# Row constants, modulation weights and the first context's keys requested ahead of the step that uses them, in a four-layer transformer kernel

## What is computed

```python
# layer 0
m = silu(mod) @ w_ada + b_ada                        # nine vectors of 256: shift, scale, gate
x = x + (window_attn(ln(x) * (1 + sc) + sh) @ w_so + b_so) * g_msa
x = x + (topk_cross(ln(x) ..., ctx @ w_kv + b_kv) @ w_co + b_co) * g_mca     # 16 largest of 77 scores
x = x + (silu(h @ m1a) * (h @ m1b) @ w_m2 + b_m2) * g_mlp
# layer 1 (512 tokens at a time)
evidence = softmax(nx @ Wq @ (proto @ Wk).T / 16) @ (proto @ Wv)
combined = concat([nx, evidence, anchor])            # the anchor is the condition, the same for all tokens
x = x + sigmoid(gate(combined)) * (sum_e p_e * expert_e(combined) @ out_w + out_b)
# layer 2
mod = cond @ adaLN_W + adaLN_b
x = x + g_msa * (masked_attn(rope(q), rope(k), v) @ attn_out_W)
x = x + g_x * (cross(xc @ cq_W, ctx @ ck_W, ctx @ cv_W, mask) @ co_W)
x = x + g_mlp * (gelu(xm @ W1 + b1) @ W2 + b2)
# layer 3
c = silu(c) @ W_mod + b_mod
x = x + gate_a * (attn(qkv + b_qkv) @ W_proj + b_proj)
x = x + (cross(...) @ W_cproj + b_cproj)
x = x + gate_m * (gelu(h @ W_mlp1 + b_mlp1) @ W_mlp2 + b_mlp2)
```

## Time and profile before

| | us |
|---|---|
| median of three runs | 3021.17 (3016.11 to 3022.32) |
| the profiled execution | 3020.91 |
| its span in the trace | 3019.6 |
| TensorE busy | 2471.6 (82%) |
| VectorE busy | 1911.2 (63%) |
| ScalarE busy | 1209.9 (40%) |
| GpSimd busy | 258.0 (9%) |

### The profile page before, as it was taken

How to read it: one execution, slowest core, us unless ns; L and a number is a source line. 1 busy time by engine, 2 the same in 40 slices (tenths; PEclk the granted TensorE clock), 3 DMA queues, 4 the chain that set the end, 5 groups by cost and what they waited for, 6 DMA issues and landing times.

```text
span 3019.6 us, 37681 instructions
## 1 busy us (share of the span) xinstructions
PE 2471.6 (82%) x13127; PEld 1252.1 (41%) x13127; DVE 1911.2 (63%) x5983; ACT 1209.9 (40%) x2250; POOL 258.0 (9%) x252
## 2 busy tenths in 40 slices
PE   5787558787699778999788989987889978889677
PEld 2455324454355353444344445442234332234335
DVE  5655857587533466556767766647777668776445
ACT  2323313343222222444434545433546626556324
POOL 2011010001210010000020010010011010000101
PEclk9798679798899796999999999997989989999869
DMA  4545141000000030000232110042220032110120
GB/s 156 146 131 150 50 128 63 20 20 13 7 7 10 30 93 17 22 11 22 72 102 75 33 27 12 12 126 70 59 42 11 28 93 80 40 25 8 56 54 14
DMA packets 151650, 161.34 MB, mean 53 GB/s; under 512 B 33471, under 2 KB 120978, under 8 KB 151196
## 3 DMA queue, kind: packets, MB, share of 16 engines
q1 hardware_dynamic: 151460, 158.94, 18.3%
HBM read 98.04 MB, written 60.19 MB: 52 GB/s over the span
## 4 chain that ended last, share of the span: by engine, by line
PE 59%; DVE 25%; ACT 5%; DMA 4%; issue 3%; POOL 2%; SPq 2%; DVEq 0%; ACTq 0%; POOLq 0%
PE bank L1097 8%; PE bank L1562 7%; PE bank L1069 6%; PE bank L1044 6%; PE bank L1583 5%; DVE max L1170 3%; PE bank L2037 3%; PE bank L722 3%; PE bank L1073 3%; DVE bank L1167 2%; PE bank L2214 2%; DVE k_stack L1334 2%; PE bank L1482 2%; PE bank L2039 1%; PE bank L663 1%
## 5 line engine op out<-in xcount | busy, mean ns | idle before, releaser
L1111 ACT ACTIVATE work<-bank 128x512 f32<-128x512 f32 (+1 forms) x1216 | 702.6, 596 | 721.7 <-PE bank L1073 296.6
L1167 DVE CUSTOM_DVE_ANT_0 bank<-bank,weights 128x512 f32<-128x512 f32 x512 | 349.1, 703 | 196.1 <-PE bank L1044 194.8
L1044 PE MATMUL bank<-k_stack,q_stack 97*128 97x512 bf16 x896 | 368.4, 413 | 89.8 <-DVE max L1167 43.4
L1170 DVE TENSOR_REDUCE max<-bank 128x1 f32<-128x512 f32 x512 | 340.8, 685 | 127.0 <-PE bank L1044 125.5
L1069 PE MATMUL bank<-q_stack,k_stack 99*128 99x512 bf16 x896 | 349.3, 393 | 15.2 <-ACT work L1111 13.0
L1562 PE MATMUL bank<-hT,weights 128*128 128x512 f32 x512 | 267.6, 623 | 15.5 <-ACT work L1608 6.8
L1044 PEld LDWEIGHTS bank<-k_stack,q_stack 97*128 97x128 bf16 x896 | 90.4, 101 | 298.6 <-DVE max L1167 118.9
L1073 PEld LDWEIGHTS bank<-ident_b,weights 128*128 128x128 bf16 x2048 | 161.0, 99 | 122.6 <-issue 15.7
L1073 PE MATMUL bank<-ident_b,weights 128*128 128x128 bf16 x2048 | 202.0, 221 | 0.0
L1583 PE MATMUL bank<-weights,work 128*128 128x256 f32 x768 | 197.8, 386 | 0.0
L1413 POOL TENSOR_TENSOR x<-x,work 128x512 f32<-128x512 f32 x64 | 82.0, 1282 | 1108.1 <-DVE work L1401 1103.6
(11 more groups left out here) (239 smaller groups left out, 3696.0 us busy)
## 6 DMA issues: line engine op xcount, KB each, us to landing
q_stack<-parts_q SPq DMA_DIRECT2D x60, 384.0 KB, 3.9
...
```

Of the source, the lines that this page charges most:

```text
L1044: m = pe.e.matmul(bank.ap[:, :], self.q(g)[0:MAX_ROW, h, qt * P:(qt + 1) * P], k_stacks[self.key, g].ap[0:MAX_ROW, h, half * BLK:(half + 1 ...
L1111: ac.e.activation(p.ap[0:self.nk, :], banks[self.key, "exp", g, i].ap[0:self.nk, :], ACT.Exp).then_inc(*probs.tick((self.key, g, i)))
L1167: ve.e.tensor_tensor_reduce(bank[:, :], bank[:, :], mask_bias[:, qt, half * BLK:(half + 1) * BLK], 1.0, -3.4e38, ALU.add, ALU.max, to).the ...
L1170: ve.e.tensor_reduce(to, bank[:, :], AX_X, ALU.max).then_inc(*maxima.tick((self.key, g, i)))
```

## The change

Two new stages exist only in SyncE's program: `Rows(stage)`, one beat, calls `load_rows` of another stage; `Ahead(mods, most)` calls `begin` and then loads one further piece in each beat, up to `most`. `OutProject.sync` is gone and `Values.sync` has become `load_rows`, so that each row of a projection and of the values is loaded where its `Rows` stands in `phases` (`early` builds one). `Mods.sync` keeps the fifth and later pieces and the store. `Mlp` and the experts keep their own loads.

In `phases` (the list starts at line 2612 now):

- the rows of `v` of sequence 0 are asked for at the start of phase 1 (counting from 0), those of `so` of sequence 0 and of `v` of sequence 1 at the start of phase 2;
- `context0` moves from the end of phase 3's second lane to the end of phase 2's, and `mods["anchor"]` the other way; `Load(["L0kv"])` moves up for it;
- the weights of the anchor, and the bias and first pieces of layers 2 and 3, have an `Ahead`;
- the rows of `co` of the first half, `so2`, `co2`, `v3` and of the last layer's `so` are asked for a stage or a phase ahead.

```diff
@@ Mods
             def sync(self, sp):
-                if self.before is not None:
-                    self.begin(sp)
-                    for p in range(1, min(4, len(self.pieces))):
-                        self.load(sp, p)
                 yield
                 for p in range(4, len(self.pieces)):
                     self.load(sp, p)
@@
+        class Ahead(Stage):
+            def __init__(self, mods, most):
+                self.mods, self.beats = mods, min(most, len(mods.pieces))
+            def sync(self, sp):
+                self.mods.begin(sp)
+                yield
+                for p in range(1, self.beats):
+                    self.mods.load(sp, p)
+                    yield
@@ Values
-            def sync(self, sp):
-                if self.bias is not None:
-                    for done, key in self.row_free:
-                        sp.wait_ge(*done[key])
-                    sp.e.dma_start(tmc[self.b][:, 1, :], self.bias.partition_broadcast(P)).then_inc(*ld_tm[self.b].tick(self.key))
-                yield
+            def load_rows(self, sp):
+                for done, key in self.row_free:
+                    sp.wait_ge(*done[key])
+                sp.e.dma_start(tmc[self.b][:, 1, :], self.bias.partition_broadcast(P)).then_inc(*ld_tm[self.b].tick(self.key))
@@
+        class Rows(Stage):
+            def __init__(self, stage):
+                self.stage = stage
+            def sync(self, sp):
+                self.stage.load_rows(sp)
+                yield
@@ OutProject
-            def sync(self, sp):
-                self.load_rows(sp)
-                yield
@@ last_stages
-            return [so, n8, xq, cross, co, n9, mlp, Store(b, mlp)], mlp.rows_left()
+            return Rows(so), [so, n8, xq, Rows(co), cross, co, n9, mlp, Store(b, mlp)], mlp.rows_left()
@@ phases
-            ([mods["L0"]], of(0, "n1", "k", "q", "v"), [Rest(3), LoadTokens(1), Rest(1)]),
-            (of(0, "win"), of(1, "n1", "k", "q", "v") + [mods["anchor"]],
-             [Rest(2), Load(["L0so", "L0q"]), Constants(), Load(["L0kv", "L0co"]), Rest(2)]),
-            (of(1, "win"), of(0, "so", "n2", "xq") + [context0], [Rest(2), load_l2, Load(["L0m1", "L0m2"]), Rest(1)]),
-            ([topk_first], of(1, "so", "n2", "xq") + [mods["L2"], mods["L3"]], [Rest(3), load_l2kv, load_l2so, load_l2q]),
+            ([mods["L0"]], [early(0, "v")] + of(0, "n1", "k", "q", "v"), [Rest(3), LoadTokens(1), Rest(1)]),
+            (of(0, "win"), [early(0, "so"), early(1, "v")] + of(1, "n1", "k", "q", "v") + [context0],
+             [Rest(1), Load(["L0kv"]), Constants(), Load(["L0so", "L0q", "L0co"]), Rest(2)]),
+            (of(1, "win"), of(0, "so", "n2", "xq") + [early(0, ("co", 0)), mods["anchor"], early(1, "so")],
+             [Rest(1), Ahead(mods["anchor"], 4), load_l2, Load(["L0m1", "L0m2"]), Rest(1)]),
+            ([topk_first], of(1, "so", "n2", "xq") + [early(1, ("co", 0)), mods["L2"], Ahead(mods["L3"], 4), mods["L3"]],
+             [Ahead(mods["L2"], 4), load_l2kv, load_l2so, load_l2q, Rest(1)]),
...
-            ([k_rows2] + of(1, ("co", 0), ("n3", 0), ("mlp", 0), ("co", 1), ("n3", 1), ("mlp", 1)), of(0, ("e", 1, "n"), ("e", 1))),
+            ([k_rows2] + of(1, ("co", 0), ("n3", 0), ("mlp", 0)) + [early(1, ("co", 1))] + of(1, ("co", 1), ("n3", 1), ("mlp", 1)),
+             of(0, ("e", 1, "n"), ("e", 1)) + [early(0, "so2")]),
             ([mask, load_l2co] + of(0, "n4", "k2", "q2", "v2") + [context2], of(1, ("e", 0, "n"), ("e", 0))),
...
-            (of(1, "self2"), of(0, "so2", "n5", "xq2", "cross2", "co2", "n6", "mlp2", "n7", "k3", "q3", "v3")),
-            (of(0, "self3"), [third] + of(1, "so2", "n5", "xq2", "cross2", "co2") + [ctx_norm, context3, v_late]
-             + of(1, "n6", "mlp2", "n7", "k3", "q3", "v3"), [load_l3m, Rest(8)]),
+            (of(1, "self2"), of(0, "so2", "n5", "xq2") + [early(0, "co2")] + of(0, "cross2", "co2", "n6", "mlp2") + [early(0, "v3")]
+             + of(0, "n7", "k3", "q3", "v3") + [rows_0]),
+            (of(0, "self3"), [third] + of(1, "so2", "n5", "xq2") + [early(1, "co2")] + of(1, "cross2", "co2") + [ctx_norm, context3, v_late]
+             + of(1, "n6", "mlp2") + [early(1, "v3")] + of(1, "n7", "k3", "q3", "v3") + [rows_11], [load_l3m, Rest(8)]),
             (of(1, "self3"), last_0),
-            (last_10, last_11),
+            ([rows_10] + last_10, last_11),
```

12 lines of the change are left out of this document (7 added, 5 removed).

## The result

The changed kernel takes 2995.77 us (median of four runs, 2991.78 to 2997.42), the kernel before 3021.74 beside it (3016.11 to 3027.01): a ratio of 0.9912, interval 0.9892 to 0.9933. The profiled execution took 2991.78 us, its span is 2990.0.

The account below looks back on a forecast made before the run. The prediction took TensorE (82% busy) and VectorE (63%) to bound the kernel, with only transfers and issuing, about 180 us, open to gains. Its parts summed to 22.6 us, 3020.9 - 22.6 = 2998.3, say 2998 us, range 2984 to 3019.

Parts of the forecast that it names:

- Part 1: Bias row of the first values, at 74 us: requested earlier, first window scores come earlier; gain 3.5 us (0 to 7.4).
- Part 2: Context keys and anchor change places: loss of 1 us around 180 us, gain of 7 around 280 us.
- The rest: Other rows put a stage ahead, where no wait shows in the trace: hidden by the attention stage beside them, costed at nothing.
- Part 3: Third layer's modulation weights requested ahead: VectorE's idle 7.10 us at 386 us shrinks; gain 6 us (3.8 to 7.1).
- rival A: Gains hidden by other waits straight after, and shifted lanes take as much as they give; 3013 us, chance 0.20.
- Part 4: Rows of the cross attention's output, first half, at 416.12 us: requested a phase ahead; gain 6.5 us (3 to 10.7).
- Part 5: The mask, issued at 977.64 us: the next projection's gate row goes ahead of it; loss 1.4 us (0 to 2.4).
- Part 6: Edge at 2010 us: 5.6 us for the gate row less 2.5 for later stacks; gain 3 us (-2.5 to 5.6).
- Part 7: Edge at 2440 us: the projection's gain is lost at later stacks; 0 us (loss of 8 to gain of 2).
- Part 8: Last phase: two more rows issued ahead of the query loads; loss 1 us (0 to 1.5).
- Rival B: SyncE's new waits hold stack loads at 180, 2010 and 2440 us, 31.5 us lost; 3032 us, chance 0.12.

Follow-up runs that it names:

- e9: The kernel before with only the bias row of the first values requested at the start of its phase; ratio 0.9997 to before.
- e10: The changed kernel with context0 given the anchor's 7 beats and the anchor the context's 12, order of transfers kept; ratio 0.9915 to before.
- e1: The changed kernel with the context's keys and the anchor back in their old phases; 2988.87 us, ratio 0.9873 to before.
- e5: The changed kernel with the last layer's projection rows requested behind the six stack loads instead of ahead; 2979.94 us, ratio 0.9877 to before.
- e8: The changed kernel with the edits of e1 and e5, and the gate row of so2 behind the mask's load; 2978.15 us, ratio 0.9863 to before.
- e11: e8 with the two bias rows of the last cross attention's output requested ahead of the query projection; 2972.77 us, ratio 0.9835 to before.
- e2: The kernel before with only the modulation weights of layers 2 and 3 requested ahead, which adds three beats; ratio 0.9935 to before.
- e3: The kernel before with four empty beats in the first top-16 phase's second lane and no transfer requested ahead; ratio 0.9941 to before.
- e4: The kernel before with only the cross attention output's two rows, first half of sequence 0, requested in the second window attention's phase; ratio 0.9977 to before.
- e0: The kernel before, unchanged, profiled once more; one run of 3017.57 us beside a median of 3025.66.

## Why the prediction was right, and where its parts were not

The time was forecast at 2998 and is 2995.77; the way of the change and its size were right, and of VectorE's waits that were named as signs those for a row (at 74, 422 and 2021 us) are gone. Part by part the sum is less good than its total.

- **Part 1** (3.5): too much. The next limit was the one named, x and the stacks: VectorE waits 5.54 us for x. But the first scores move by 1.7 to 2.5 us, starts taken off (e9 1.7, changed kernel 1.9), and in the changed kernel that is lost in the window stage.
- **Part 2** (-1 and +7): wrong in sum, and in sign. The edge at 180 us itself is near the forecast: the stacks leave at 184.54 (estimated 188), the first scores come at 192.43 (estimated 193), and the table has 1.8 us lost. But "a loss of 1, as four us of matrix work leave this edge too" left no room for what else was won before it: TensorE stands 8.80 us, and whatever makes the window stage shorter ends in that wait, in e10 9.3 us, just beyond my bound of 8.3. The other step that failed was not in the text at all: a context of 12 beats in place of an anchor of 7 re-deals the window stage and costs 7 us. At 280 us the idle time for queries went, and most of the gain with it: the last shift rows came behind six stores, and the anchor filled the rest. I had allowed "2 to 4" of the anchor's 8.5 and put the first scores at 282 to 285; they came at the same time as before, 289.25 against 289.40. Together the exchange costs about 3 us where 6 were booked as won (e1, e5, e8, e11).
- **The rest** (0): "rows put a stage ahead where no wait for them shows in the trace" was a misreading. VectorE's waits of 5.55, 5.47 and 7.39 us for the values' rows were there. The first is part of the 6 us by which e1 is ahead of e9 at 165 us; the second bounded nothing (e8, in which it is gone, stays 36.6 us ahead from 1984 to 2012 us); with the third gone e5 and e8 move 5 us ahead between 2430 and 2450, and the changed kernel, 5 us ahead too, gives them to the wait for the key stack. None of the three rows was moved alone.
- **Part 3** (6): the stretch gained 12.7 in the changed kernel (355 to 412 us), and on top of the added beats the weights are worth some 3 of it (e2 less e3). The mechanism, TensorE no longer waiting for the weight, was there, but 9 us are had by the order of the lanes alone, which the forecast had only in rival A, as a loss. Of VectorE's wait of 7.10 us 3.27 are left, now for TensorE's matmuls alone (369.25 in the changed kernel), so the wait itself gave 3.8, the lower bound. Those matmuls' 3.6 us were their time at a granted clock of 0.50; at full clock they take 1.88.
- **Part 4** (6.5): right. 6.3 in the changed kernel (392 to 432), 5.6 alone (e4).
- **Part 5** (-1.4): the sign was right, the size low: -2.9, over the bound of 2.4, and e8 gives it back.
- **Part 6** (3): 0.5. The step "the first full score moves to about 2017" was off: the wait for the key stack grew by 4.4 us, not by 2.5, and against the work before it the score comes 4.0 us later, over the 3 us that the forecast had named as a sign of being wrong. With the rows behind the stacks the whole 6 are there (e5).
- **Part 7** (0): -1, and 3 are to be had (e5). **Part 8** (-1): -4.5 at its place (16.48 against 11.98 us of idle time). The table has 6.8 there because sixteen matmuls ahead of it took 9.41 us instead of 7.16, and 5.9 of the 6.8 are regained by the end.

Rival B described the losses well in mechanism and at its three edges, if not in size (9.3, 5.6 and 4.0 us by e10 and e5, 31.5 in my worst case), but was not the whole: 9 us of interleaving that no part had foreseen, and the sound part 4, outweighed them. The total was right by luck, because errors of opposite sign cancel: up to 355 us 4.7 were gained of a booked 9.5, at 355 to 432 us 19.0 of a booked 12.5, and at the places of parts 5 to 8 4.3 were lost where 0.6 was booked as won. That makes 19.4. The remaining 10 us, up to the 29.5 of the two traces, lie in the long attention stages. Part of them is the granted clock, as between 1150 and 1250 us. The rest stays open: between 1090 and 2000 us the changed kernel gains 16.5 us, 6.7 of them in TensorE's busy time, where e1 gains 9.1, e5 6.2 and e0 1.5.

The fixed cost of a transfer by the Trainium skill, "DMA: Bandwidth & Descriptors", "Anatomy of one DMA", would have given part 4 about 2.3 us; it gave 6.3, and was rightly set aside there.
